# One recurrent product per time step, issued as four products of 32 output rows

## The chip, the cores and the metric

The program runs on one core of a Trainium2 chip. The metric is the device time of one execution in microseconds (us), median over runs. TensorE (PE in the rows; PEld is its weight load) multiplies, VectorE is DVE, ScalarE is ACT, GpSimd is POOL, SyncE (SP) issues the DMAs. PSUM is the memory that TensorE writes its results to.

## The reference

The input is x of shape (8, 512, 128): batch 8, sequence 512, width 128. First comes a recurrent layer, then six layers of windowed attention and feed-forward. The change touches the recurrent layer alone:

```python
xb = jnp.einsum('bsd,ed->sbe', x, B)          # x here is layernorm(input)
def step(h, xb_t):
    h = jnp.tanh(h @ A.T + xb_t)
    y = h @ C.T
    return (h, y)
_, ys = jax.lax.scan(step, h0, xb)            # 512 steps, each needs the h of the one before
out = jnp.transpose(ys, (1, 0, 2)) + x        # then layernorm(out) * gamma + beta, added to the input
```

A, B and C are 128 by 128, h is 8 by 128, all float32. Then six times: x = attention(shift(x)) + x, x = feed_forward(shift(x)) + x.

## The kernel before

**Recurrent layer.** The 512 time steps are cut into NC = 8 chunks of FW = 64 steps. For a chunk c, TensorE first writes B times the normalised inputs of all its 64 steps into one PSUM bank (L480, one float32 product with 512 columns, called the input product here). Then comes the loop over t (L482). Each of its 512 passes through the two loops, called a step here, does this: TensorE waits for the h of the step before (semaphore `h_done`), multiplies A by it (L485; 128 output rows, contraction over 128, 8 columns, one for each sequence of the batch) and adds the result to the 8 columns of the step in PSUM; it signals `pre_done`. ScalarE waits for that and takes the tanh (L688) into `hb`, which signals `h_done`. That is a closed ring of two engines: product, tanh, product.

**Filler.** After each such product TensorE issues two matmuls of bf16, 128 by 128 with 512 columns (`keep_warm`, L469), whose result nobody reads. They stand between the product of a step and that of the next. Here they are called the fillers.

**Extra work in the loop.** TensorE's queue also carries, between two steps: at t = 3 the product of the last chunk with C (`outputs`, L458, four float32 products of 128 columns), at t = 38 four transposes of that chunk's result (`turn_input`, L465), at t = 54 four transposes of the next chunk's normalised input (`turn_xn`, L451). ScalarE copies what the transposes leave (L681 and L677) between two of its tanhs. VectorE's normalisations run beside the loop.

**The six layers.** After the loop a software pipeline of 192 tiles runs (`step(s)`): q, k and v products (L502), transposes (L509), similarities (L643, products on a quarter of the array's columns and half its rows, 64 by 32), weighted sums (L657, 32 by 128), output product (L597), layer products of weights (L608, 64 by 128), feed-forward (L537 to L551). Its similarities come behind two bf16 matmuls that write the mask (L636, the same form as a filler). Nothing in this part is touched.

**How a float32 product shows.** Each float32 matmul appears in the trace as two passes: weight load, matmul, weight load, matmul. A bf16 matmul is one weight load and one matmul. Each queue is in program order, written out by hand; no scheduler moves anything. A weight load carries the wait of its matmul. The tile names in the rows are those of memory that is shared: `cosp` and `qT` at L485 are the state h and the matrix A.

Of the kernel before, what the change touches and what calls it, by code (L numbers as in the profile page):

```python
# [24 lines left out]
P = 128  # L25
BATCH, SEQ, D = 8, 512, 128
# [5 lines left out]
FW = 64  # L32
# [72 lines left out]
def build(nc, a):  # L105
    with ExitStack() as ctx:
# [3 lines left out]
        def sem(name):  # L110
            return ctx.enter_context(nc.semaphore(name))
# [59 lines left out]
        abcT = qT[:, 3:6, :]  # L171
# [6 lines left out]
        ps = ctx.enter_context(nc.psum_tensor("ps", [P, 8, 512], F32))  # L178
# [17 lines left out]
        pre_done = sem("pre_done")  # L196
# [95 lines left out]
        def after(eng, signal, value):  # L292
            if value > 0:
                eng.wait_ge(signal, value)
# [146 lines left out]
        def _(eng):  # L441
# [5 lines left out]
            def turn_xn(c):  # L447
                eng.wait_ge(ln1_step, LN_STEPS * (c + 1))
                after(eng, xn_out, c)
                for j in range(TB):  # L450
                    t = eng.transpose(ps[:, 3, P * j:P * j + P], xn_tm[:, c % 2, j, :], ident[:, :])  # L451
                t.then_inc(ln1_turned, 1)

            def outputs(c):
                eng.wait_ge(hs_done, c + 1)
                after(eng, post_step, POST_STEPS * c)
                for j in range(TB):
                    t = eng.matmul(ps[:, 4, P * j:P * j + P], hs[:, P * j:P * j + P], abcT[:, 2, :], start=True, stop=True)  # L458
                t.then_inc(hs_turned, 1)

            def turn_input(c):
                eng.wait_ge(post_step, POST_STEPS * (c + 1))
                after(eng, x_updated, c)
                for j in range(TB):
                    t = eng.transpose(ps[:, 5, P * j:P * j + P], lnd[:, j, :], ident[:, :])  # L465
                t.then_inc(post_turned, 1)

            def keep_warm():
                eng.matmul(ps[:, 7, 0:KEEP].rearrange("p (a n) -> p a n", n=P), ident_bf[:, :],  # L469
                           ident_bf[:, :].unsqueeze(1).to_broadcast([P, KEEP // P, P]), start=True, stop=True)  # L470
# [5 lines left out]
            for c in range(NC):  # L476
                r = c % 2
                after(eng, h_done, FW * c)
                eng.wait_ge(xn_out, c + 1)
                eng.matmul(ps[:, r, :], abcT[:, 1, :], xn_fm[:, r, :].rearrange("p (b t) -> p t b", b=BATCH),  # L480
                           start=True, stop=False, skip_group_check=True).then_inc(pre_started, 1)
                for t in range(FW):  # L482
                    after(eng, h_done, FW * c + t)
                    prev = hb[:, r, t - 1, :] if t else hb[:, 1 - r, FW - 1, :]
                    eng.matmul(ps[:, r, BATCH * t:BATCH * t + BATCH], abcT[:, 0, :], prev, start=False, stop=t == FW - 1,  # L485
                               skip_group_check=True).then_inc(pre_done, 1)
                    keep_warm()
                    keep_warm()
                    if t == AT_OUTPUT and c:
                        outputs(c - 1)  # L490
                    if t == AT_INPUT and c:
                        turn_input(c - 1)
                    if t == AT_XN and c < NC - 1:
                        turn_xn(c + 1)
# [525 lines left out]
```

## Time and profile before

| | |
|---|---|
| median of 3 runs | 3785.27 us (3783.42 to 3791.43) |
| profiled execution, its own time | 3787.83 us |
| profiled execution, span | 3786.0 us |
| mean granted TensorE clock | 0.969 |
| PE busy | 3558.4 us (94%) |
| first and last weight load of the product with A | 18.5 us and 382.7 us |

The profiled execution agrees with the median within 0.1%. The recurrent loop fills the first tenth of the span; the six layers fill the rest. A matmul's row in the trace starts when the array begins to take its columns, or earlier, while its weights still load, and ends when its result is out, so rows of consecutive matmuls overlap and a busy share of 94% is not 94% of the array's peak.

### The profile page before, as it was taken

What the parts mean: (1) busy time and instruction counts of PE and PEld (TensorE: products, weight loads), DVE (VectorE), ACT (ScalarE), POOL (GpSimd) and SP (SyncE); (2) the same over time, 40 slices, a digit from 0 to 9 for tenths busy, and PEclk for the clock granted to TensorE, in tenths of its full rate; (3) what the DMA queues carried; (4) which work ended last, traced back from release to release, by engine and by line L of the source; (5) the groups of instructions that cost most, each with busy time, mean ns of one, the idle gap of its engine ahead of it and who ended that gap; (6) DMA issues with size and microseconds to landing.
All of it is one profiled execution on the core that took longest, in us unless ns stands there. A gap on an engine that the chain in (4) does not pass through costs nothing.

```text
span 3786.0 us, 101581 instructions
## 1 busy us (share of the span) xinstructions
PE 3558.4 (94%) x42643; PEld 2250.6 (59%) x42643; DVE 3058.2 (81%) x5670; ACT 2037.8 (54%) x3871; POOL 2086.7 (55%) x1217
## 2 busy tenths in 40 slices
PE   8999699999999999999999999999999999999997
PEld 4555366666665666666665666666656666566664
DVE  3443698888898888888888898888888888888884
ACT  2222356565565565565655655656556556556553
POOL 0000376666566666666665666666666666666662
PEclk9999899999999999999999999999999999999998
DMA  2000000000001000001000001000001000000000
GB/s 66 1 1 1 7 10 12 28 10 10 9 14 32 10 10 7 10 16 29 10 10 10 7 16 32 10 7 10 10 15 31 10 10 7 14 12 16 10 10 12
DMA packets 62283, 52.55 MB, mean 14 GB/s; under 512 B 11526, under 2 KB 59396, under 8 KB 61828
## 3 DMA queue, kind: packets, MB, share of 16 engines
q1 hardware_dynamic: 61828, 46.05, 4.6%
q8 instruction: 338, 5.54, 0.6%
q14 instruction: 117, 0.96, 0.1%
HBM read 43.93 MB, written 2.10 MB: 12 GB/s over the span
## 4 chain that ended last, share of the span: by engine, by line
PE 62%; DVE 19%; issue 11%; POOL 5%; ACT 2%; DVEq 0%; DMA 0%; SPq 0%; POOLq 0%; ACTq 0%
PE ps L502 16%; PE ps L597 12%; PE ps L657 7%; PE ps L469 6%; PE ps L509 6%; DVE sinp L848 4%; DVE mx L938 3%; PE ps L643 3%; PE ps L551 3%; DVE pT L921 3%; PE ps L485 3%; PE ps L537 3%; POOL cosp L424 2%; POOL cosp L414 2%; DVE ss L854 2%
## 5 line engine op out<-in xcount | busy, mean ns | idle before, releaser
L414 POOL TENSOR_TENSOR cosp<-cosp,rr 128x1024 f32<-128x1024 f32 x384 | 722.5, 1902 | 823.1 <-DVE rr L65 823.0
L424 POOL TENSOR_TENSOR cosp<-cosp,sinp 128x1024 f32<-128x1024 f32 x384 | 904.7, 2368 | 96.1 <-DVE sinp L848 95.5
L502 PE MATMUL ps<-w_qk,xs 128*128 128x512 f32 x1536 | 814.9, 656 | 19.8 <-ACT sq L709 14.2
L597 PEld LDWEIGHTS ps<-px,w_vo 128*128 128x128 f32 x6144 | 729.5, 197 | 155.2 <-issue 118.7
L597 PE MATMUL ps<-px,w_vo 128*128 128x128 f32 x6144 | 739.6, 280 | 22.9 <-issue 18.4
L709 ACT ACTIVATE sq<-ps 128x1024 f32<-128x1024 f32 x384 | 393.1, 1024 | 571.3 <-DVE sinp L848 571.3
L845 DVE TENSOR_TENSOR cosp<-ps,tab 128x1024 f32<-128x1024 f32 x384 | 469.6, 1223 | 267.6 <-PE ps L502 267.4
L749 ACT COPY px<-ps 128x512 f32<-128x512 f32 x768 | 398.8, 598 | 431.0 <-PE ps L657 428.2
L657 PE MATMUL ps<-pT,xtm 32*128 32x512 f32 x3072 | 539.6, 629 | 88.3 <-DVE hh L869 74.7
L502 PEld LDWEIGHTS ps<-w_qk,xs 128*128 128x128 f32 x1536 | 279.9, 203 | 403.5 <-issue 401.8
L854 DVE TENSOR_REDUCE ss<-sq 128x16 f32<-128x1024 f32 x384 | 455.6, 1187 | 60.9 <-ACT sq L709 60.5
L848 DVE TENSOR_TENSOR sinp<-ps,tab 128x1024 f32<-128x1024 f32 x384 | 466.3, 1214 | 0.0
L509 PEld LDWEIGHTS ps<-ident,cosp 128*128 128x128 f32 x3072 | 352.2, 142 | 159.4 <-issue 101.0
L509 PE MATMUL ps<-ident,cosp 128*128 128x128 f32 x3072 | 403.4, 275 | 43.5 <-POOL cosp L414 31.1
L419 POOL TENSOR_TENSOR pn<-ex,rsum 128x1024 f32<-128x1024 f32 x192 | 365.1, 1902 | 98.1 <-DVE rsum L909 98.1
L657 PEld LDWEIGHTS ps<-pT,xtm 32*128 32x128 f32 x3072 | 202.1, 184 | 274.4 <-DVE hh L869 113.2
L775 ACT COPY kT<-ps 128x512 f32<-128x512 f32 x384 | 206.1, 589 | 279.4 <-PE ps L509 279.4
L643 PEld LDWEIGHTS ps<-kT,qT 64*32 64x32 f32 x24576 | 254.6, 105 | 84.5 <-issue 78.0
L469 PE MATMUL ps<-ident_bf 128*128 128x512 bf16 x1024 | 303.8, 377 | 0.0
L643 PE MATMUL ps<-kT,qT 64*32 64x64 f32 x24576 | 286.0, 226 | 2.2 <-ACT kT L775 2.1
L485 PEld LDWEIGHTS ps<-cosp,qT 128*128 128x128 f32 x1024 | 154.0, 189 | 166.4 <-ACT cosp L688 156.1
L921 DVE STREAM_TRANSPOSE pT<-pn 128x1024 f32<-128x1024 f32 x192 | 237.0, 1234 | 3.5 <-POOL pn L419 3.5
(101 smaller groups left out, 4094.2 us busy)
## 6 DMA issues: line engine op xcount, KB each, us to landing
tab<-in_tab SPq DMA_DIRECT2D x96, 128.0 KB, 2.0
qks<-in_scales SPq DMA_DIRECT2D x96, 128.0 KB, 3.2
w_qk<-in_L_ffn_Wqkv SPq DMA_DIRECT2D x12, 512.0 KB, 6.9
w_v<-in_wv_t SPq DMA_DIRECT2D x6, 512.0 KB, 8.7
w_o<-in_L_ffn_Wo SPq DMA_DIRECT2D x6, 512.0 KB, 9.1
x<-in_L_attn_x SPq DMA_DIRECT2D x16, 128.0 KB, 3.4
out<-w_v SPq DMA_DIRECT2D x16, 128.0 KB, 2.4
w<-in_L_ffn_W SPq DMA_DIRECT2D x6, 341.0 KB
```

Of the source, the lines that this page charges most:

```text
L414: eng.tensor_tensor(v, v, rr[:, B % 2, HEADS * i:HEADS * i + HEADS].unsqueeze(2).to_broadcast([P, HEADS, DH]), ALU.mult).then_inc(rot_read ...
L424: eng.tensor_tensor(cosp[:, A % 2, i, :], cosp[:, A % 2, i, :], sinp[:, i, :], ALU.add).then_inc(rot_added, 1)
L469: eng.matmul(ps[:, 7, 0:KEEP].rearrange("p (a n) -> p a n", n=P), ident_bf[:, :], ident_bf[:, :].unsqueeze(1).to_broadcast([P, KEEP // P, ...
L502: t = eng.matmul(ps[:, u, :], xs[:, n % ROUND, :], w_qk[:, n // TILES % 2, i, 512 * u:512 * u + 512], start=True, stop=True)
L509: t = eng.transpose(G(k)[:, 128 * m:128 * m + 128], cosp[:, n % 2, i, at:at + 128], ident[:, :])
L597: t = eng.matmul(S0, w_vo[:, i // HP, i % HP, :], px[:, i, :], start=i == 0, stop=i == HEADS - 1)
L643: t = eng.matmul(ps[32 * b:32 * b + 32, 2 + h2, DH * hp:DH * hp + DH], qT[rows, hp, 32 * b:32 * b + 32], kT[rows, B % NG, hp, b, :], start ...
L657: t = eng.matmul(G(b), xtm[rows, C % NG, k, :], pT[rows, :].rearrange("p (h k q) -> p h k q", k=2, q=WIN)[:, :, k, :], start=k == 0, stop= ...
L749: eng.copy(px[:, :, 32 * b:32 * b + 32], G(b).rearrange("p (h q) -> p h q", q=WIN)).then_inc(px_evac, 1)
L845: eng.tensor_tensor(cosp[:, n % 2, i, :].rearrange("p (h d) -> p h d", d=DH), src, cos, ALU.mult).then_inc(roped, 1)
L848: eng.tensor_tensor(sinp[:, i, :].rearrange("p (h u f) -> p h u f", u=2, f=32), swapped, sin, ALU.mult).then_inc(roped, 1)
L854: eng.tensor_reduce(ss[:, HEADS * i:HEADS * i + HEADS], sq[:, i, :].rearrange("p (h d) -> p h d", d=DH), AX_X, ALU.add).then_inc(ssq_done, 1)
```

## The change

In the loop over t the one matmul with 128 output rows becomes four with 32 output rows each. Each takes 32 columns of the transposed A as its weights and the same 128 by 8 moving operand, and writes its own 32 partitions of PSUM. Only the last of the four signals `pre_done`; the first carries the wait for `h_done`.

```diff
                 for t in range(FW):
                     after(eng, h_done, FW * c + t)
                     prev = hb[:, r, t - 1, :] if t else hb[:, 1 - r, FW - 1, :]
-                    eng.matmul(ps[:, r, BATCH * t:BATCH * t + BATCH], abcT[:, 0, :], prev, start=False, stop=t == FW - 1,
-                               skip_group_check=True).then_inc(pre_done, 1)
+                    for f in range(0, P, 32):
+                        m = eng.matmul(ps[f:f + 32, r, BATCH * t:BATCH * t + BATCH], abcT[:, 0, f:f + 32], prev, start=False, stop=t == FW - 1,
+                                       skip_group_check=True)
+                    m.then_inc(pre_done, 1)
                     keep_warm()
                     keep_warm()
```

TensorE's queue at the border of two chunks, before (L480 is the input product, L485 the product with A, L469 the fillers):

```order
L485 MATMUL ps<-cosp,qT 128x8 [waits h_done]
L469 MATMUL ps<-ident_bf 128x512 x2
L480 MATMUL ps<-cosp,qT 128x512 [waits xn_out,h_done]
L485 MATMUL ps<-cosp,qT 128x8 [waits h_done]
L469 MATMUL ps<-ident_bf 128x512 x2
```

and the same place with the change (the product is now at L486):

```order
L486 MATMUL ps<-cosp,qT 32x8 [waits h_done]
L486 MATMUL ps<-cosp,qT 32x8 x3
L469 MATMUL ps<-ident_bf 128x512 x2
L480 MATMUL ps<-cosp,qT 128x512 [waits xn_out,h_done]
L486 MATMUL ps<-cosp,qT 32x8 [waits h_done]
L486 MATMUL ps<-cosp,qT 32x8 x3
L469 MATMUL ps<-ident_bf 128x512 x2
```

Nothing has changed places; every product with A is four in a row, with the wait on the first.

TensorE's queue around t = 3 of a chunk, before (L458 is the product with C):

```order
L485 MATMUL ps<-cosp,qT 128x8 [waits h_done]
L469 MATMUL ps<-ident_bf 128x512 x2
L458 MATMUL ps<-qT,px 128x128 [waits hs_done]
L458 MATMUL ps<-qT,px 128x128 x3
L485 MATMUL ps<-cosp,qT 128x8 [waits h_done]
L469 MATMUL ps<-ident_bf 128x512 x2
```

and with the change:

```order
L486 MATMUL ps<-cosp,qT 32x8 [waits h_done]
L486 MATMUL ps<-cosp,qT 32x8 x3
L469 MATMUL ps<-ident_bf 128x512 x2
L458 MATMUL ps<-qT,px 128x128 [waits hs_done]
L458 MATMUL ps<-qT,px 128x128 x3
L486 MATMUL ps<-cosp,qT 32x8 [waits h_done]
L486 MATMUL ps<-cosp,qT 32x8 x3
L469 MATMUL ps<-ident_bf 128x512 x2
```

The four small products here follow the product with C, as the one large product did.

## Rows read from the trace of the kernel before

**Rows 1.** The page: busy time of each engine; granted clock in 40 slices.
```profile
PE 3558.4 (94%) x42643; PEld 2250.6 (59%) x42643; DVE 3058.2 (81%) x5670; ACT 2037.8 (54%) x3871; POOL 2086.7 (55%) x1217
PEclk9999899999999999999999999999999999999998
```

**Rows 2.** Windows, loop and the rest: PE, PEld, DVE, ACT, POOL busy, clock, DMA.
```profile
18.50:383.50 365.00, 362.37 (x2176) 192.68 (x2174) 135.65 (x404) 97.51 (x526) 8.14 (x8) 1.00 0.03 9
383.50:3786.00 3402.50, 3192.97 (x40460) 2056.19 (x40460) 2915.07 (x5244) 1937.99 (x3342) 2074.25 (x1201) 0.97 0.05 14
```

**Rows 3.** Lines L485 and L469: ns min/median/max; then idle before L485, us, times.
```profile
L485 PEld LDWEIGHTS ps<-cosp,qT x1024: 185/189/337, 18.5 to 382.7; 128*128 128x128 f32 x171
L485 PE MATMUL ps<-cosp,qT x1024: 174/257/362, 19.4 to 382.7; 128*128 128x8 f32 x171
...
  ACT cosp L688: 158.7, 497
...
L469 PE MATMUL ps<-ident_bf x1024: 375/377/635, 19.6 to 383.1; 128*128 128x512 bf16 x171
```

**Rows 4.** Timeline of the loop: start us, us, engine line, xcount [idle before <-releaser].
```profile
300.34 0.18 ACT L688 ACTIVATE cosp<-ps 128x8 f32<-128x8 f32 x1 [0.48 <-PE ps L485]
...
302.34 0.38 PE L469 MATMUL ps<-ident_bf 128*128 128x512 bf16 x1
302.53 0.19 PEld L485 LDWEIGHTS ps<-cosp,qT 128*128 128x128 f32 x1 [0.31 <-ACT cosp L688]
302.64 0.19 PEld L485 LDWEIGHTS ps<-cosp,qT 128*128 128x128 f32 x1
302.67 0.26 PE L485 MATMUL ps<-cosp,qT 128*128 128x8 f32 x1
302.78 0.59 PE L469 MATMUL ps<-ident_bf 128*128 128x512 bf16 x2
302.96 0.18 ACT L688 ACTIVATE cosp<-ps 128x8 f32<-128x8 f32 x1 [0.48 <-PE ps L485]
303.19 0.19 PEld L485 LDWEIGHTS ps<-cosp,qT 128*128 128x128 f32 x1 [0.31 <-ACT cosp L688]
...
310.17 0.18 ACT L688 ACTIVATE cosp<-ps 128x8 f32<-128x8 f32 x1 [0.48 <-PE ps L485]
```

**Rows 5.** Timeline in the six layers: four places where the matmul form changes.
```profile
1001.30 0.38 PE L636 MATMUL ps<-mask,ident_bf 128*128 128x512 bf16 x1
1001.61 0.10 PEld L643 LDWEIGHTS ps<-kT,qT 64*32 64x32 f32 x1 [0.42 <-issue]
...
2372.92 0.45 PE L643 MATMUL ps<-kT,qT 64*32 64x64 f32 x23
2373.30 0.18 PEld L657 LDWEIGHTS ps<-pT,xtm 32*128 32x128 f32 x1
...
512.96 1.07 PE L657 MATMUL ps<-pT,xtm 32*128 32x512 f32 x8
513.96 0.19 PEld L502 LDWEIGHTS ps<-w_qk,xs 128*128 128x128 f32 x1 [0.76 <-issue]
...
1531.87 0.27 PE L601 MATMUL ps<-ident,xs 128*128 128x128 f32 x1
1532.07 0.30 PEld L608 LDWEIGHTS ps<-w_o,w_v 64*128 64x128 f32 x4 [0.17 <-issue]
```

**Rows 6.** Timeline, 50 ns at the first similarities; the page's row of their matmuls.
```profile
1001.61 0.15 PEld L643 LDWEIGHTS ps<-kT,qT 64*32 64x32 f32 x12 [0.42 <-issue]
...
L643 PE MATMUL ps<-kT,qT 64*32 64x64 f32 x24576 | 286.0, 226 | 2.2 <-ACT kT L775 2.1
```

**Rows 7.** Timeline of the loop at t = 54 and at t = 3 of a chunk.
```profile
101.75 0.60 PE L451 MATMUL ps<-ident,cosp 128*128 128x128 f32 x4
103.10 0.39 PE L485 MATMUL ps<-cosp,qT 128*128 128x8 f32 x2 [0.18 <-ACT cosp L688]
...
112.75 1.05 PE L458 MATMUL ps<-qT,px 128*128 128x128 f32 x8
113.78 0.38 PE L469 MATMUL ps<-ident_bf 128*128 128x512 bf16 x1
```

## The prediction

> **What bounds the kernel now.** I read the windows first. The loop over the 512 steps spans 365 of 3786 us at a granted clock of 1.00, that is 2.4 GHz, and all other engines are mostly idle in it: VectorE 136 us, ScalarE 98, GpSimd 8 [rows 2]. The six layers take the other nine tenths at a mean clock of 0.97 [rows 1, 2]; no instruction there changes. So the change is worth what it does to one step, times 512.
>
> Next the timeline of the loop. Between the tanh at 300.34 and that at 310.17 lie 15 steps, so one takes 9.83 / 15 = 0.655 us [rows 4]. Inside one: first weight load at 302.53, second at 302.64, its matmul ends at 302.67 + 0.26 = 302.93, the tanh runs from 302.96 to 303.14, and the next weight load starts at 303.19. Load to result 0.39-0.40, tanh and two signals 0.26: the ring closes at 0.655, and the product's load waits for the tanh in 497 cases [rows 3, 4]. So the ring of latencies is the bound.
>
> How near is TensorE's own queue? The two fillers start 0.59 - 0.377 = 0.215 apart [rows 3, 4], which is the time that 512 columns take. The second one of the step before starts at 302.34, so its columns are in at 302.555. The load of 302.53 is under way by then, hidden in a spare set of weights. 128 float32 columns take 0.11 to load (the two loads start so far apart), until 302.64. Thus a filler that ended up to 0.085 later would cost nothing; more than that would.
>
> **The change part by part.** Removed are 512 products with 128 output rows, added 2048 with 32: per step 2 weight loads and 2 matmuls become 8 and 8. Two things follow.
>
> (1) The product itself gets shorter. A weight load's row is its loading and a fixed 0.08 (0.19 - 0.11). A load of 32 float32 columns shows 0.10 in the similarities [rows 5], so it loads for 0.02 to 0.03; I take a quarter of 0.11, 0.027. Twelve such loads start within 0.15 - 0.10 = 0.05 us, on different parts of the array [rows 6]. Eight loads for four column strips should thus start within about 0.05. The last is loaded at about 0.075, and a matmul of 8 columns ends some 0.175 after its weights are in (302.93 against 302.64 + 0.11 = 302.75). The result stands 0.25 after the first load, not 0.39-0.40: the ring of latencies alone would fall from 0.655 to about 0.51.
>
> (2) TensorE must change its form twice a step: from 128 by 128 (fillers) to 128 by 32 and back. What that costs stands in the six layers, at four places with four pairs of forms [rows 5]. The filler-like L636 ends at 1001.30 + 0.38 = 1001.68, the first load of the next form starts at 1001.61. L643 ends at 2373.37, the load of L657 starts at 2373.30. L657 ends at 514.03, the load of L502 starts at 513.96. L601 ends at 1532.14, that of L608 starts at 1532.07. Always 0.07 before the end of the old form's last matmul, at whatever length of matmul, so it is no semaphore. Within one form a load starts far earlier: 303.19, with the second filler ending at 303.37, 0.18 before the end, and only because the tanh came no sooner [rows 4]. So after a change of form nothing is preloaded: the next load starts 0.377 - 0.07 = 0.307 after the start of the last filler, or 0.09 after its last column is in.
>
> One step with both changes: second filler starts at 0; first small load at 0.307; last small result 0.25 later at 0.557; the filler's load 0.07 before that, at 0.487; its weights need about 0.03 (its first columns follow the second product's load by that: 302.64 + 0.11 = 302.75, filler at 302.78); first filler at 0.517; second filler 0.215 later. Sum 0.732; I take 0.730. The ring of latencies, 0.51, is done long before and is no longer the bound. Bounds from the same rows: 0.724 if the eight small matmuls leave the array as soon as their 8 columns are through, 0.743 if each strip needs 0.027 for a matmul of 8 columns (second matmul's row at 302.67, weights of the first in at 302.64 [rows 4]). So +0.069 to +0.088 per step, +0.075 taken.
>
> Some steps are not of that kind [rows 7]. At t = 54 and 38 four transposes of the fillers' form and a copy on ScalarE come between; step 55 then waits for ScalarE (the product at 103.10 does). The last small result is no longer what is late there, and the fillers start 0.03 earlier after the product than before: those two steps and their followers (28 of 511 distances) lose nothing, together some -0.5 us. At t = 3 the product with C fills the queue from 112.75 to the end of its columns at about 113.64. Before, the product's first load lay under it and the filler followed at 113.78, 0.14 after; now 0.09 + 0.18 + 0.03 = 0.30 after. With the step behind it that is +0.24, seven times +1.7. The chunk border (input product) gives +0.08 for two steps, seven times +0.5. The remaining 455 steps: 455 x 0.075 = 34.1. Sum 34.1 - 0.5 + 1.7 + 0.5 = 35.8 us; bounds 33 and 42.
>
> What else could move: the recurrence's end moves by that sum and the six layers start as much later, unchanged. VectorE's normalisations of 136 us lie in a loop that only gets longer. Nothing is hidden and nothing new is waited for.
>
> The profiled execution took 3787.8 itself, so 3823.6; from the median 3785.3, which is what is measured, 3821.
>
> The Trainium skill, page "TensorEngine Tiling (Array Packing)", section "Key Properties", says that changing the tiling mode, not just the tile, drains TensorE. No row here shows the very change of this case, where only the column division changes (all four places also change the rows). By this rule it costs as much as the others, and the sum stands; without it, the first rival below would be the result.
>
> **Rivals.**
>
> *No drain where only the columns are divided.* Against: L643 also divides columns and pays. For: in all four places the rows' division changes too, so none isolates it. Then small loads slip under the filler, and TensorE needs per step the fillers 0.43, eight small passes about 0.08-0.10 and the filler's load 0.03: 0.54-0.56, above the ring's 0.51. 455 x -0.105 = -48 us, the pairs with extra work give back about 1: near 3737. This is the case on the other side; it decides as soon as the two changes of form together cost less than 0.11 instead of 0.18 per step.
>
> *Drain in one direction only.* 0.730 - 0.092 = 0.638: 455 x -0.017 = -8, so 3777.
>
> *The eight small passes don't overlap.* For: only products of half the rows (64 by 32) were seen side by side; over the whole run they take 286.0 us / 24576 = 0.012 apiece [rows 6], but 128-row strips might load one after another. Eight times 0.027 is 0.22 instead of 0.075: +0.14 per step on top, 0.87 in all, 512 x 0.215 = +108 with 3893 as the end; half of it (loads overlap a little) gives 3857.
>
> The skill's page "TensorE: Matmul & The Clock Gate", section "Wait — 56ns, not 53.3ns?", gives a floor of about 25 ns from matmul to matmul, however few columns. By it eight small ones would take 0.2 and the time would be near this rival's. The 0.012 apiece of the rows speaks against it for matmuls on different strips.
>
> *The clock falls.* Fillers fill 0.43 of 0.73 us instead of 0.43 of 0.655. The loop has 1.00 throughout, the six layers 0.97 with lower slices [rows 1, 2]. At the lower level, 1.2 GHz, a filler's columns take twice as long; its slowest row, 0.635 instead of 0.377 [rows 3], is 0.26 more, as half the clock would give. Two of them and the drains make a step at least 0.55 longer. A tenth of the loop in that state would be +28, all of it +280.
>
> **How the numbers follow.** Forecast, 3818 to 3828: 0.66. No drain: 0.11. One direction: 0.07. No overlap: 0.11. Clock: 0.05. The range 3775 to 3868 holds the forecast, the one-direction case and the half of the no-overlap case: 0.66 + 0.07 + 0.06 = 0.79. A change of this kernel can be told from none at about 0.2%, 7.6 us. Faster by more: no drain and half of the one-direction case, 0.15. Within: the other half and a little, 0.04. Slower: 0.81.
>
> **What would show it.** In the profile after: tanhs 0.73 apart in the loop; the first small load 0.31 after the second filler's start and 0.07 before its end, with idle time before it put down to no engine; the filler's load 0.07 before the end of the last small matmul; tanh starting 0.29 after the first small load, and ready 0.2 before the next product takes it; eight small loads starting within 0.05; granted clock 1.00 in the loop; the six layers as long as before, 3402.5 us. Wrong would be: small loads starting under the filler's columns (then the time falls), small loads 0.03 apart (then it is near 3857 to 3893), a clock under 1.00.

## The result, and the profile after

| | before | changed |
|---|---|---|
| median | 3785.3 us (3783.42 to 3791.43) | 3821.65 us (3820.01 to 3822.32) |
| ratio | | 1.0093, 95% interval 1.0075 to 1.011 |
| profiled execution, its own time and span | 3787.83, 3786.0 | 3822.32, 3820.5 |

The forecast was 3821, with 3775 to 3868 around it. The median is within 1 us of it, and that is better than the working deserves. Between the two profiled executions the loop grew by 29.7 us, where 35.8 were forecast, and the six layers by 4.8 us, where nothing was. The medians differ by 36.4 and not by the sum of 34.5, because the profiled execution of the kernel before was itself 2.5 us above its median.

The windows of the changed kernel, loop and rest (columns as in [rows 2]):

```profile
20.10:413.20 393.10, 392.56 (x5238) 155.11 (x5236) 134.48 (x403) 97.50 (x526) 8.14 (x8) 1.00 0.03 9
413.20:3820.50 3407.30, 3196.92 (x40461) 2055.93 (x40460) 2914.83 (x5244) 1937.88 (x3342) 2074.59 (x1201) 0.96 0.05 14
```

The stretch before lasted 365 and 3402.5 us [rows 2]. In the same cut, from the last tanh on, the rest is 3786.0 - 383.0 = 3403.0 before and 3820.5 - 412.7 = 3407.8 after; the last tanh moved by 29.7. VectorE, ScalarE and GpSimd do the same work in the same time in both stretches.

One step of the changed kernel, in its timeline (L486 is the product with A, L690 the tanh):

```profile
174.16 0.16 PEld L486 LDWEIGHTS ps<-cosp,qT 128*32 128x32 f32 x8 [0.42 <-ACT cosp L690]
174.16 0.25 PE L486 MATMUL ps<-cosp,qT 128*32 128x8 f32 x8
174.34 0.10 PEld L469 LDWEIGHTS ps<-ident_bf 128*128 128x128 bf16 x1
174.48 0.18 ACT L690 ACTIVATE cosp<-ps 128x8 f32<-128x8 f32 x1 [0.54 <-PE ps L486]
174.57 0.38 PE L469 MATMUL ps<-ident_bf 128*128 128x512 bf16 x1
174.88 0.16 PEld L486 LDWEIGHTS ps<-cosp,qT 128*32 128x32 f32 x8 [0.42 <-ACT cosp L690]
...
184.51 0.18 ACT L690 ACTIVATE cosp<-ps 128x8 f32<-128x8 f32 x1 [0.54 <-PE ps L486]
```

Fourteen steps lie between the tanhs of 174.48 and 184.51: 10.03 / 14 = 0.716 us each (0.717 in the median), where it was 0.655 [rows 4]. The eight loads span 0.16 from the first start to the last end, and the product's result is out 0.25 after the first load (0.39-0.40 before). The filler's load starts at 174.34, 0.07 before the product's end at 174.41. The second filler ends at 174.57 + 0.38 = 174.95, and the next product's load starts at 174.88, 0.07 before that. The tanh ended at 174.66; the next product could have started at 174.71, as the ring before shows (303.14 to 303.19 in [rows 4]), and starts at 174.88. The page puts this idle time down to the tanh, because that is the last signal which the load waited for. But the tanh had been done for 0.22 us. This is a case where the named releaser is not the cause. The prediction had expected the page to name no engine here.

The product's line in numbers (columns as in [rows 3]), with the idle time that the page puts down to the tanh:

```profile
L486 PEld LDWEIGHTS ps<-cosp,qT x4096: 106/109/154, 19.7 to 412.5; 128*32 128x32 f32 x196
L486 PE MATMUL ps<-cosp,qT x4096: 176/197/223, 19.7 to 412.5; 128*32 128x8 f32 x196
...
  ACT cosp L690: 206.9, 483
```

The ends of matmuls in the trace are modelled and the starts are recorded. So here is the same once more by starts, from the whole trace: the first small load comes 0.308 us after the start of the second filler (512 columns), and the filler's load 0.104 after the start of the last small matmul (8 columns). Put against the recorded ends, the filler's load lies 0.071 to 0.072 before the end of the last small matmul in all 512 steps, and the small product's load lies as far before the end of the second filler in 97% of the 483 steps in which it follows one.

### The profile page after: what moved, and what is told of

Same layout as the page of the kernel before. It is cut to its first block, busy times and chain, and to the rows that moved or that the text cites. A ratio compares the mean times of both kernels' runs of the same rounds, so it can differ in the third digit from the quotient of the medians.

```text
span 3820.5 us, 107725 instructions
## 1 busy us (share of the span) xinstructions
PE 3593.8 (94%) x45715; PEld 2213.1 (58%) x45715; DVE 3057.9 (80%) x5670; ACT 2037.7 (53%) x3871; POOL 2087.0 (55%) x1217
## 4 chain that ended last, share of the span: by engine, by line
PE 63%; DVE 19%; issue 11%; POOL 5%; ACT 2%; DVEq 0%; DMA 0%; SPq 0%; POOLq 0%; ACTq 0%
PE ps L504 16%; PE ps L599 12%; PE ps L659 7%; PE ps L469 7%; PE ps L511 6%; DVE sinp L850 4%; DVE mx L940 3%; PE ps L645 3%; PE ps L553 3%; DVE pT L923 3%; PE ps L539 3%; PE ps L486 2%; POOL cosp L424 2%; POOL cosp L414 2%; DVE ss L856 2%
## 5 line engine op out<-in xcount | busy, mean ns | idle before, releaser
L469 PE MATMUL ps<-ident_bf 128*128 128x512 bf16 x1024 | 310.5, 385 | 0.0
L690 ACT ACTIVATE cosp<-ps 128x8 f32<-128x8 f32 x512 | 90.8, 177 | 287.1 <-PE ps L486 287.1
```

## The experiments

All are timed against the kernel before, whose median over their runs was 3785 to 3786. "Loop" is first to last tanh in the profiled execution, "rest" the last tanh to the end.

| | step, us | loop | rest | median | ratio (95%) |
|---|---|---|---|---|---|
| before | 0.655 | 363.2 | 3403.0 | 3785.3 | |
| changed | 0.717 | 392.7 | 3407.8 | 3821.7 | 1.0093 (1.0075-1.011) |
| e1, fillers in strips | 0.545 | 317.2 | 3401.1 | 3741.6 | 0.9882 (0.9857-0.9907) |
| e2, one strip added to before | 0.768 | 451.4 | 3398.4 | 3861.7 | 1.0197 (1.0155-1.0238) |
| e3, changed, short fillers | 0.545 | 320.7 | 3401.0 | 3746.8 | 0.9897 (0.9876-0.9918) |
| e4, before, short fillers | 0.860 | 459.3 | 3411.3 | 3886.7 | 1.0267 (1.0244-1.0289) |
| e5, two strips of 64 | 0.757 | 435.7 | 3396.9 | 3842.2 | 1.015 (1.0127-1.0173) |
| e6, short after the first chunk | 0.545 | 310.4 | 3392.9 | 3728.9 | 0.9852 (0.9832-0.9872) |
| e7, the same, all in strips | 0.545 | 312.4 | 3403.8 | 3734.6 | 0.9863 (0.9847-0.9879) |
| e8, third filler in before | 0.655 | 364.8 | 3401.5 | 3788.7 | 1.0004 (0.9993-1.0016) |

**e1: no change of form.** From the changed kernel:

```diff
-                eng.matmul(ps[:, 7, 0:KEEP]..., ident_bf[:, :],
-                           ident_bf[:, :].unsqueeze(1)..., start=True, stop=True)
+                for f in range(0, P, 32):
+                    eng.matmul(ps[f:f + 32, 7, 0:KEEP]..., ident_bf[:, f:f + 32],
+                               ident_bf[:, :].unsqueeze(1)..., start=True, stop=True)
```

> The changed kernel, but each filler is issued as four matmuls of 128 by 32 with 512 columns, one for each column strip: the same columns streamed, and no change of form between product and fillers. Theory (the two changes of form cost the time): both 0.09 us waits go, small loads slip under the fillers, and a step falls from 0.717 to about 0.52 us, bounded by the fillers' 0.43 and some 0.09 of passes, or by the ring of latencies (0.51). Against the kernel before (0.655): 455 x -0.13 = about -60 us, near 3725, ratio 0.984. Rival (the extra instructions of the small products cost the time, not the change of form): fillers of four matmuls make it worse still, 0.72 or more a step, at 3822 or above. A second rival: bf16 strips do not run side by side, a filler takes 4 x 0.215, a step over 1.8 us, +590 us.

Measured: 3741.6. This is the experiment that isolates the change of form: the product is that of the changed kernel, the fillers stream their 512 columns in the same time, there are six more matmuls a step, and the kernel is 80 us faster than the changed one. Its timeline in the loop (L487 product, L470 fillers, L691 tanh):

```profile
250.06 0.16 PEld L487 LDWEIGHTS ps<-cosp,qT 128*32 128x32 f32 x8 [0.34 <-ACT cosp L691]
250.06 0.25 PE L487 MATMUL ps<-cosp,qT 128*32 128x8 f32 x8
250.11 0.14 PEld L470 LDWEIGHTS ps<-ident_bf 128*32 128x32 bf16 x8
250.14 0.61 PE L470 MATMUL ps<-ident_bf 128*32 128x512 bf16 x8
250.37 0.18 ACT L691 ACTIVATE cosp<-ps 128x8 f32<-128x8 f32 x1 [0.37 <-PE ps L487]
250.60 0.16 PEld L487 LDWEIGHTS ps<-cosp,qT 128*32 128x32 f32 x8 [0.34 <-ACT cosp L691]
```

The fillers' loads start at 250.11, while the product's own loads still run, and the next product's loads start at 250.60, 0.15 before the fillers end at 250.75. The tanh ended at 250.55, so this load really waits for it. The step is the ring of latencies, 0.545, and not the 0.52 expected; over 455 steps that is 11 of the 17 us by which the time lies above the expected 3725. The second rival fell too: eight matmuls in strips take 0.61, as two whole ones do.

**e2: a change of form alone.** From the kernel before:

```diff
+                    eng.matmul(ps[0:32, 7, 0:8], ident_bf[:, 0:32], ident_bf[:, 0:8], start=True, stop=True)
                     keep_warm()
                     keep_warm()
```

> The kernel before with its whole 128-row product, and one added bf16 matmul of 128 by 32 with 8 columns (result read by nobody) between the product and the fillers: the change of form alone. Theory: the small load starts 0.07 before the end of the product, the filler's load 0.07 before the end of the small one; TensorE's queue needs 0.28 (second pass of the product out) - 0.07 + 0.20 (small one) - 0.07 + 0.017 + 0.215 + 0.215 = about 0.79 us a step and is the bound: +0.13 x 455 to 511 = +60 to +67 us, near 3850, ratio 1.017. Rival (change of form costs nothing here, the eight passes of the small products do): one more small matmul hides under the ring's slack of 0.08, and the time stays 3785.

Measured: 3861.7, slower than expected, with single runs from 3844.5 to 3875.3. Its timeline:

```profile
300.64 0.09 PEld L487 LDWEIGHTS ps<-ident_bf 128*32 128x32 bf16 x1
300.75 0.11 PEld L469 LDWEIGHTS ps<-ident_bf 128*128 128x128 bf16 x2
300.98 0.41 PEld L485 LDWEIGHTS ps<-cosp,qT 128*128 128x128 f32 x2
301.41 0.09 PEld L487 LDWEIGHTS ps<-ident_bf 128*32 128x32 bf16 x1
...
61.10 0.18 ACT L689 ACTIVATE cosp<-ps 128x8 f32<-128x8 f32 x1 [1.14 <-PE ps L485]
62.41 0.18 ACT L689 ACTIVATE cosp<-ps 128x8 f32<-128x8 f32 x1 [1.14 <-PE ps L485]
```

From 300.64 to 301.41 a step takes 0.77 (median 0.768), 0.113 more than before, for one tiny matmul that nobody waits for. The theory said 0.79. The product's load at 300.98 lies under the fillers, with which it shares its form. In the profiled execution there is a second effect of 29 us: the first 54 steps take 1.31 each (61.10 to 62.41), 54 x 0.545 = 29. Their fillers run at half speed:

```profile
61.12 1.03 PE L469 MATMUL ps<-ident_bf 128*128 128x512 bf16 x2
```

Two of them take 1.03 here and 0.59 to 0.61 at 2.4 GHz. How long this lasted in the other three executions is not known; it may be why they differ by 31 us. More on this below.

**e3 and e4: shorter fillers.** In each the same edit, `KEEP = 512` to `KEEP = 256`; e3 from the changed kernel, e4 from the one before.

> The changed kernel with fillers of 256 columns instead of 512. Theory (TensorE's queue is the bound after the change, ring of latencies 0.514 below it): the queue needs 0.717 - 0.215 = 0.502, so the ring 0.250 + 0.037 + 0.177 + 0.050 = 0.514 takes over; a step falls to about 0.515 while the granted clock stays 1.00: about -103 against the changed kernel, -72 against the one before, near 3715, ratio 0.981. Rival (the ring of latencies is longer with small products and is the bound): no change from 3822. Rival on the clock: shorter fillers let it fall to 1.2 GHz in the loop; then a step is 0.6 or more and the gain is gone.

> The kernel before with fillers of 256 columns instead of 512. Theory (before the change the ring of latencies is the bound, 0.655, and the fillers lie in its slack): a step stays 0.655, only the 28 to 42 steps with extra work on TensorE get shorter by up to 0.2 each; 3778 to 3785, ratio 0.998 to 1.000, if the clock stays 1.00. Rival (TensorE's queue is the bound before as well): a step falls by 0.215, to 0.44, -100 us. Rival on the clock: it falls in the loop, product and fillers take longer, and a step goes to 0.75 or more, +50 us.

e3 measured 3746.8, where 3715 was expected. Its queue would allow 0.502, and the step is 0.545, as in e1. So the ring of latencies with four strips is 0.545, 0.031 longer than reckoned, which makes 14 us over 455 steps. A slow start, as in e2, makes another 12 (56 steps of 0.767). The timeline of e3 shows both the plain steps and the start of the loop:

```profile
300.26 0.25 PE L486 MATMUL ps<-cosp,qT 128*32 128x8 f32 x8
300.44 0.39 PE L469 MATMUL ps<-ident_bf 128*128 128x256 bf16 x2
300.58 0.18 ACT L690 ACTIVATE cosp<-ps 128x8 f32<-128x8 f32 x1 [0.37 <-PE ps L486]
300.81 0.25 PE L486 MATMUL ps<-cosp,qT 128*32 128x8 f32 x8
...
40.23 0.61 PE L469 MATMUL ps<-ident_bf 128*128 128x256 bf16 x2
40.76 0.30 PE L486 MATMUL ps<-cosp,qT 128*32 128x8 f32 x8
40.99 0.61 PE L469 MATMUL ps<-ident_bf 128*128 128x256 bf16 x2
```

The product ends at 300.51 and its tanh starts at 300.58, 0.066 by the medians, where the whole product has 0.037 (302.93 to 302.96 in [rows 4]). At 40 us two fillers of 256 columns take 0.61; at 300 us they take 0.39. They run at half speed there.

e4 measured 3886.7: the clock rival came true in it. The row of its page, and two windows:

```profile
PEclk9555589999999999999999999999999999999999
```

```profile
65.00:200.00 135.00, 133.98 (x643) 86.89 (x642) 41.15 (x120) 28.74 (x153) 3.39 (x3) 0.61 0.00 1
200.00:300.00 100.00, 99.32 (x474) 65.12 (x474) 36.95 (x113) 21.40 (x116) 1.13 (x1) 0.54 0.00 1
```

A mean of 0.5 to 0.6 is the clock at its lower level, 1.2 GHz, most of the time, and a step is 0.860. In the short stretches at 2.4 GHz its steps are 0.655, as with full fillers, which is the ring of latencies:

```profile
82.30 0.18 ACT L688 ACTIVATE cosp<-ps 128x8 f32<-128x8 f32 x1 [0.48 <-PE ps L485]
82.96 0.18 ACT L688 ACTIVATE cosp<-ps 128x8 f32<-128x8 f32 x1 [0.48 <-PE ps L485]
```

So the kernel before needs the full length of its fillers for its clock, and at 2.4 GHz they cost its plain steps nothing.

**e5: two strips of 64.** From the changed kernel:

```diff
-                    for f in range(0, P, 32):
-                        m = eng.matmul(ps[f:f + 32, ...], abcT[:, 0, f:f + 32], ...)
+                    for f in range(0, P, 64):
+                        m = eng.matmul(ps[f:f + 64, ...], abcT[:, 0, f:f + 64], ...)
```

> The changed kernel with two products of 64 output rows in place of four of 32. Theory: the two changes of form cost the same, and only the small products' own time grows. A load of 64 float32 columns takes 0.054, two passes 0.107, the second strip starts 0.007 later, a result 0.176 after its weights: last end 0.290 after the first load (0.250 with four). A step is 0.309 + 0.290 - 0.072 + 0.231 = 0.758 us (0.717 with four), 455 x 0.041 = +19 against the changed kernel, near 3840, ratio to the kernel before 1.014. The tanh starts 0.066 after the last end with four strips and 0.037 with the whole product; if that grows with the number of matmuls side by side it is about 0.05 here, if it is due to the form it is 0.066. Rival (the number of instructions costs the time): half as many, so faster than the changed kernel, near 3803.

Measured: 3842.2 and a step of 0.757, against 0.758 expected. A kernel with half as many small products is slower, so it is not their number that costs the time; the sum with the longer weight load fits to 0.001. One step in its timeline:

```profile
310.19 0.29 PE L486 MATMUL ps<-cosp,qT 128*64 128x8 f32 x4
310.41 0.11 PEld L469 LDWEIGHTS ps<-ident_bf 128*128 128x128 bf16 x2
310.53 0.18 ACT L690 ACTIVATE cosp<-ps 128x8 f32<-128x8 f32 x1 [0.58 <-PE ps L486]
```

Product 0.29, the filler's load 0.07 before its end, the tanh 0.046 after it (median). With 0.037, 0.046 and 0.066 for one, two and four matmuls side by side, the wait for the result is longer by some 0.01 for each one added. It is no fixed price of dividing the array, which would be the same for two and four; whether it goes by the number of strips or by their width no run separates, and as the ends are modelled, part of it may lie in the model. This execution too began with half-speed steps, 1.29 us each up to 77 us, which is why its loop is 43 us longer than the changed kernel's and not 19. It was the slowest of the four (3835.6 to 3853.9). That the median came out 20.5 above the changed kernel's, near the 19 of the theory, is thus in part luck; what shows the theory is the step.

**e6 and e7: the way out.** From the changed kernel; e6 takes strips for the fillers only in the first chunk, e7 in all:

```diff
-                    keep_warm()
-                    keep_warm()
+                    for _ in range(2):
+                        if c:
+                            keep_warm(256, False)    # e7: True
+                        else:
+                            keep_warm(KEEP, True)    # True: four matmuls of 128 by 32
```

> The changed kernel with fillers of 256 whole-form columns from the second chunk on, and in the first chunk fillers of 512 columns in strips. Theory: with short fillers in the first chunk the loop began at 1.2 GHz, 56 steps of 0.767 us; with full ones it has 2.4 GHz from the start and 0.545 a step, and once it is there short ones hold it. Loop 321 - 56 x 0.22 = 309 us, near 3733, ratio 0.986. Rival: the clock falls once the fillers get short, steps of 0.77, the loop at 370 us or more, near 3800.

> All fillers in strips, so product and fillers have one form: 512 columns in the first chunk, 256 after it. Theory: plain steps stay at 0.545, the ring of latencies; TensorE's queue is far below it. What falls is the extra work's steps (t = 3, 38, 54), by the 0.2 of the shorter fillers, seven times each, and not below what the change of form to transposes and products with C costs: loop 317 - 21 x 0.2 = 313 us, near 3737, ratio 0.987. Rival: with no change of form TensorE has less to do and the clock falls, 0.7 or more a step, 3800 or above.

Measured: 3728.9 and 3734.6, where 3733 and 3737 were expected, and the best of all. The windows of e6:

```profile
19.90:330.30 310.40, 305.88 (x5622) 150.09 (x5614) 134.45 (x403) 97.71 (x526) 7.86 (x7) 1.00 0.04 11
330.30:3723.20 3392.90, 3182.36 (x40462) 2051.24 (x40460) 2914.33 (x5244) 1939.36 (x3343) 2075.49 (x1201) 0.97 0.05 14
```

The loop is 53 us shorter than in the kernel before, at a clock of 1.00. Part of e6's lead over e7 is its rest, shorter by 11 us, in which the two kernels do the same; by loop alone they are 2 us apart. In e6 the two changes of form are still paid, but they lie in TensorE's slack, since its queue is now 0.502 and the ring 0.545.

**e8: the slack of the kernel before.** One more filler of 128 columns ahead of the two:

```diff
+                    keep_warm(P)
                     keep_warm()
                     keep_warm()
```

> The kernel before with one more filler of 128 columns ahead of the two of 512. Theory (0.085 us of slack on TensorE before the change): its 0.054 fits, a step stays at 0.655, only the 21 steps with extra work and the chunk borders grow by 0.05: 3785 to 3787, ratio 1.000. Rival (TensorE's queue already is as late as the ring): +0.054 a step, 512 x 0.054 = +28, near 3813.

Measured: 3788.7, ratio 1.0004, an interval that holds 1. Its timeline:

```profile
300.29 0.18 ACT L689 ACTIVATE cosp<-ps 128x8 f32<-128x8 f32 x1 [0.48 <-PE ps L485]
300.52 0.30 PEld L485 LDWEIGHTS ps<-cosp,qT 128*128 128x128 f32 x2 [0.26 <-ACT cosp L689]
300.60 0.31 PE L485 MATMUL ps<-cosp,qT 128*128 128x8 f32 x2
300.77 0.65 PE L469 MATMUL ps<-ident_bf 128*128 128x128 bf16 x3
300.95 0.18 ACT L689 ACTIVATE cosp<-ps 128x8 f32<-128x8 f32 x1 [0.48 <-PE ps L485]
```

The matmul's row starts at 300.60, 0.075 after its load instead of 0.02, because the fillers' columns run that long; its weights are in only at 300.63. The step stays 0.655. So the slack on TensorE was there, and the changes of form were more than it could hold. Beside e2 this is the plainest comparison: one more matmul of 128 columns in the fillers' form costs nothing, and one more of 8 columns in another form costs 0.113 us a step.

## Why the prediction was right

**The bound before** was the ring of latencies, with 0.085 us of slack on TensorE: e8 used 0.054 of it at no cost, and e4's steps at full clock are 0.655 with half the fillers.

**Term (1), the product gets shorter**: 0.25 forecast, 0.25 measured. The rival by which the eight passes don't overlap fell: eight loads span 0.16, of which one is 0.106. The floor of about 25 ns from matmul to matmul in the Trainium skill (page "TensorE: Matmul & The Clock Gate", section "Wait — 56ns, not 53.3ns?") does not hold across strips in this trace: the first four matmuls of the product start 0.005 to 0.007 apart.

**Term (2), the changes of form**: 0.307 from the second filler to the next load and 0.07 before the product's end to the filler's load, both as forecast. The trace thus shows what [rows 5] could not, a change in the column division alone, 128 by 128 to 128 by 32 and back, and it costs the same as the others. The rule of the Trainium skill (page "TensorEngine Tiling (Array Packing)", section "Key Properties") that a change of mode drains TensorE agrees with this: the 0.07 is there in both directions. That this is the cause is shown by e1, which takes it away and is 80 us faster, and by e2, which adds it to the kernel before and is slower. e8 beside e2 shows that it isn't the added matmul as such. The two rivals, no drain and a drain in one direction, fell. So did the clock's: the granted clock is 1.00 in the loop, and two fillers take 0.60 to 0.61, as in e2 and e5 at 2.4 GHz.

**The term that was mis-sized** is the filler's weight load after the product. I allowed 0.03 from load to first column, so 0.245 to the second filler; the rows give 174.57 - 174.34 = 0.23. That makes 0.717, not 0.730, and over 455 steps 28.2 instead of 34.1 us. Both lie outside my own bounds: the lower one was 0.724 for a step and 33 us for the loop. The price was read from a filler's load that stood behind the product's second load (302.64 to 302.78 in [rows 4]); here, where no load runs before it, it is about 0.015.

One slip in the sums changes nothing: 512 x 0.215 is 110 us and not 108, so the rival with no overlap should have stood at 3895.

**The steps with extra work** were right in sum. From tanh to tanh, seven of each: t = 3 1.462 to 1.608 with its follower 0.655 to 0.716, together +0.207 (forecast +0.24); t = 38 with its follower 2.027 to 1.978, -0.05 (at t = 54 the same), where 0.035 less was forecast; the chunk border +0.086 (forecast +0.08). At t = 54, for example:

```profile
109.14 0.60 PE L451 MATMUL ps<-ident,cosp 128*128 128x128 f32 x4
109.67 0.25 PE L486 MATMUL ps<-cosp,qT 128*32 128x8 f32 x8
109.85 0.39 PE L469 MATMUL ps<-ident_bf 128*128 128x512 bf16 x1
```

The transposes end at 109.74, and the product starts 0.07 before; in [rows 7] it could preload under them.

**The ring of latencies** with small products was forecast at 0.51 and is 0.545 (e1, e3), by the result's later signal. In the changed kernel this is hidden behind TensorE's queue. It would have made the rival without a drain 0.545 as well, inside its 0.54 to 0.56. The same term was a sign in the prediction, the tanh 0.29 after the first small load; it starts 0.317 after it.

**The six layers** were forecast as unchanged. They do the same work, but last 3392.9 to 3411.3 us in the ten profiled executions of the table, with nothing in them changed. Their granted clock drops at places that vary, to a mean of 0.96 or 0.97. The 4.8 us that they added between the two profiles are well inside this scatter, though no run shows that they are chance and no effect of the change. They made up for most of the 6 us by which the loop was overestimated, and the 1.9 us between the difference of the medians and that of the profiles did the rest. The exact hit is thus partly luck; the sign of the loop's growth, and its size to a fifth, are not.

## What to carry to other kernels

Before splitting a product into strips, look at what stands before and after it on TensorE: each change of form costs about 0.09 us after the last column and takes away the preloading of weights. Split only where the neighbours have the same form, or where the queue has slack for two such waits: the same split that cost 36 us here gained 44 once the fillers were strips too (e1), and 51 with these strips cut to half from the second chunk on (e7). With the slack, whole fillers cut to half from the second chunk on, it gained 57 (e6). And where the trace names a releaser, check that it had not ended long before.

## What the runs showed of the hardware

- A change of form, that is of how the array is divided into halves or quarters, cost the same for every pair seen: the next weight load starts 0.07 us before the recorded end of the last matmul of the old form, after 8 columns as after 512. It comes later only where something else holds it up.
- Not every change of shape is such a change. In the six layers 128 by 128 stands next to 128 by 85 and 85 by 128, and there the load starts 0.59 before the recorded end, as between two equal float32 products of 512 columns. In the kernel before (the two matmuls end at 674.72):

```profile
673.70 1.02 PE L544 MATMUL ps<-xf,w 128*128 128x512 f32 x2
674.13 0.15 PEld L544 LDWEIGHTS ps<-xf,w 128*85 128x85 f32 x1 [0.24 <-issue]
```

- The wait from a product's recorded end to the tanh that reads it was 0.037, 0.046 and 0.066 us with one, two and four matmuls side by side. Why is open.
- In the profiled executions of e2, e3, e4 and e5 the loop began at half speed, with fillers of 512 columns in e2 and e5. The recorded clock rose at 95 us in e2, 65 in e3, 79 in e4 and 77 in e5. In the other kernels it rose by 23 us. In e3 the slow steps were 0.767 instead of 0.545, in e2 1.31 instead of 0.768. In e2 and e3 the rise came within 4 us after the transposes of t = 54, in e4 just after the first chunk border, in e5 between plain steps; what decides it is open. The clock column shows 1.00 in those stretches, since the record of the clock starts only with its first change. It is the doubled filler rows that show it. In e2, from 19 to 65 us (columns as in [rows 2]):

```profile
19.00:65.00 46.00, 46.00 (x175) 31.53 (x173) 4.34 (x16) 6.05 (x34) 0.00 (x0) 1.00 0.21 60
```

- e3 and e4 have the same fillers. Once the clock is up, it stays up through the rest of the loop in e3, with a step of 0.545, and falls again and again in e4, with a step of 0.655. A filler can be shortened without loss only as far as the clock holds, and that is seen in the granted clock of the run alone.
